# Value products of two softmax attentions: v stationary in column tiles instead of p, with p normalized on GpSimd

## What is computed

```python
# third layer ("wide"): 16 heads of 64
q = (xn @ w_q); k, v = split(context @ w_kv)
scores = einsum('bqhd,bkhd->bhqk', q * SCALE, k)
attn = softmax(scores, axis=-1)
out = einsum('bhqk,bkhd->bqhd', attn, v).reshape(B, SQ, INNER)
out = (out @ w_out + b_out) * tanh(gate[0])
# fourth layer ("narrow"): 16 heads of 16, with a mask
q = query @ Wq.T + bq;  k = key @ Wk.T + bk;  v = value @ Wv.T + bv
scores = where(mask == 0, -1e9, q @ k.T / sqrt(16))
out = softmax(scores) @ v
out = out @ Wo.T + bo
```

## Time and profile before

| | us |
|---|---|
| median of 3 runs | 3672.95 |
| lowest and highest run | 3671.74 and 3675.34 |
| the profiled execution: its own time | 3672.53 |
| the profiled execution: its span | 3670.8 |
| one full wide batch, from scores to scores (1692.84 to 1744.00) | 51.16 |
| one full narrow batch (3101.91 to 3131.27) | 29.36 |

### The profile page before, as it was taken

One profiled execution on the slowest core, in us unless ns is written; L12 is line 12 of the kernel. 1 busy time (PEld: TensorE's weight loads), 2 busy tenths in 40 slices (PEclk: granted clock), 3 DMA queues, 4 the chain that ended last, 5 costly groups with the idle time before them and its releaser, 6 DMA issues. The chain is left out here.

```text
span 3670.8 us, 48289 instructions
## 1 busy us (share of the span) xinstructions
PE 2872.7 (78%) x15310; PEld 2137.1 (58%) x15310; DVE 1500.6 (41%) x5309; ACT 1074.4 (29%) x2159; POOL 292.5 (8%) x338
## 2 busy tenths in 40 slices
PE   4774189996699979699999999927997199999232
PEld 3663167775466745456666666626886077777121
DVE  5886312222211123423333333430111666666777
ACT  3442011110355421033334333302221044444121
POOL 0000300002311100000000000021001211110000
PEclk8896589998799879899999999958998599999555
DMA  2111132211111100100000000025553100000000
GB/s 73 42 48 60 36 139 92 76 61 35 54 34 33 34 30 0 55 9 9 5 8 8 8 8 4 1 88 183 179 180 118 54 26 18 18 18 7 23 0 20
DMA packets 62362, 174.11 MB, mean 47 GB/s; under 512 B 13387, under 2 KB 32601, under 8 KB 52793
## 3 DMA queue, kind: packets, MB, share of 16 engines
q1 hardware_dynamic: 52184, 148.10, 12.2%
q0 software_dynamic: 10080, 24.79, 2.2%
HBM read 143.50 MB, written 29.36 MB: 47 GB/s over the span
## 5 line engine op out<-in xcount | busy, mean ns | idle before, releaser
L2077 PE MATMUL L_ffne_up<-L_ffne_xT,L_ffne_wu 128*128 128x280 f32 (+1 forms) x1696 | 406.1, 398 | 23.1 <-DVE L_ffne_xT L2003 15.6
L2077 PEld LDWEIGHTS L_ffne_up<-L_ffne_xT,L_ffne_wu 128*128 128x128 f32 x1696 | 324.9, 193 | 94.7 <-ACT L_ffne_hT L1990 16.7
L1212 PEld LDWEIGHTS L_xattn_o<-L_xattn_v,L_xattn_pt 125*112 125x112 f32 x3072 | 335.8, 178 | 42.2 <-issue 14.8
L1212 PE MATMUL L_xattn_o<-L_xattn_v,L_xattn_pt 125*112 125x64 f32 (+1 forms) x3072 | 328.2, 251 | 0.0
L1063 DVE TENSOR_REDUCE L_xattn_least<-L_xattn_s 112x1 f32<-112x375 f32 x256 | 128.4, 543 | 473.0 <-PE L_xattn_s L1192 472.8
L2063 PE MATMUL L_ffne_dn<-L_ffne_wd,L_ffne_hT 128*128 128x256 f32 (+1 forms) x1312 | 288.0, 379 | 1.6 <-issue 1.6
L1199 PEld LDWEIGHTS L_xattn_pt<-ident,L_xattn_p 112*125 112x125 f32 x1536 | 186.7, 188 | 138.0 <-issue 138.0
L2063 PEld LDWEIGHTS L_ffne_dn<-L_ffne_wd,L_ffne_hT 128*128 128x128 f32 (+1 forms) x1312 | 240.8, 184 | 44.7 <-issue 2.4
L1147 PE MATMUL L_xattn_job<-L_xattn_ctxT,L_xattn_wk 128*128 128x375 f32 x640 | 233.0, 493 | 2.2 <-DMA L_xattn_msk<-in_mask 1.0
L1076 DVE COPY L_xattn_pt<-L_xattn_pt 125x336 f32<-125x336 f32 x512 | 234.2, 499 | 1.0 <-PE L_xattn_pt L1199 1.0
L1199 PE MATMUL L_xattn_pt<-ident,L_xattn_p 112*125 112x112 f32 x1536 | 232.2, 287 | 0.0
(11 more groups left out here) (318 smaller groups left out, 3875.4 us busy)
## 6 DMA issues: line engine op xcount, KB each, us to landing
L_ffne_wd<-in_L_ffn_down SPq DMA_DIRECT2D x29, 1024.0 KB, 4.9
L_ffne_wu<-in_L_ffn_up SPq DMA_DIRECT2D x21, 1024.0 KB, 5.4
L_ffne_wu<-in_L_ffn_up SPq DMA_DIRECT2D x8, 2048.0 KB, 8.0
L_xattn_ctxT<-in_ctxT SPq DMA_DIRECT2D x32, 375.0 KB, 3.1
fa_ctxT<-in_ctxT SPq DMA_DIRECT2D x16, 375.0 KB, 6.1
fa_rows<-in_ctx_rows SPq DMA_DIRECT2D x16, 375.0 KB
ta_kT<-in_ctxT SPq DMA_DIRECT2D x16, 375.0 KB
ta_ctxr<-in_ctx_rows SPq DMA_DIRECT2D x16, 375.0 KB
```

What stands on the lines that cost most here:

```text
L1212: m = pe.matmul(o, pt_sb[:, head % 4, kt, :], v_sb[:, h, kt, hd, :], start=(kt == 0), stop=(kt == KT - 1))
L2077: m = pe.matmul(up_ps[s % RING][k][:, 0, 0:RH], wu[:, h, c, k * FF + f * 128:k * FF + (f + 1) * 128], xT[:, h, c, q * RH:(q + 1) * RH], st ...
```

## The change

Products are turned round. v of a head is now the stationary operand (125 x 64 in the wide part, 125 x 32 in the narrow part, whose 16 columns are padded with zeros to 32), and `pt` moves with 112 columns. The output of a head is transposed, head columns by queries, and goes to partitions that start at a multiple of 64 or 32: two heads (wide) or four (narrow), `SIDE`, write side by side into column tiles of the array. The tile `o` is then already `onT` for the output projection: `take_o` on ACT copies it, and the transposes of `on` and `head_mean` are gone. As the sum belongs to a query, which is now a column, p is divided before its transpose: the exponential gives the sum, `invert` on DVE takes 1/sum for a pair, and POOL multiplies both heads' p by it, after an instruction on one element. `turn_p` waits for POOL. LT is 4 and LP is 6 (wide) or 8 (narrow), and the rings of p and pt hold 8 heads. In the narrow part `onT` has four chunks of 128 rows instead of two (padding), so the output projection has four matmuls instead of two, and the bias of v goes once through the output projection into `bias_y`.

```diff
-    LT = 2
-    LP = 4
+    LT = 4
+    LP = 6 if wide else 8
+    RP = 8
     if wide:
-        slots = [[K[0]], [K[1]], [K[2], K[3]], [K[4]], [K[5]], [O[0]], [O[1], K[6]], [K[7]], [Y], [Q[0]], [Q[1]],
+        slots = [[K[0]], [K[1]], [K[2]], [K[3]], [K[4]], [K[5], K[6]], [K[7]], [], [Q[0]], [Q[1]], [Y],
                  [V[0]], [V[1], V[2]], [V[3]], [V[4], V[5]], [X]]
     else:
-        slots = [[K[0]], [], [K[1]], [], [Q[0]], [], [O[0]], [], [Y], [], [V[0]], [], [V[1]], [], [X], []]
+        slots = [[K[0]], [], [K[1]], [], [Q[0]], [], [V[0]], [], [V[1]], [], [Y], [], [V[2]], [], [X], []]
...
+                def body(b, h):
+                    for pair in range(0, H, 2):
+                        if pair == 10 and not wide and exists(b + 1):
+                            prepare(b + 1, 1 - h)
+                        pool.wait_ge(rec_done, b * H // 2 + pair // 2 + 1)
+                        pool.tensor_tensor(core.pool_tick[:, pair:pair + 1], ident[0:1, 0:1], ident[0:1, 0:1], ALU.mult)
+                        for head in (pair, pair + 1):
+                            p = pool.tensor_scalar(p_sb[:, head % RP, :], p_sb[:, head % RP, :],
+                                                   rec[:, h, head:head + 1], None, ALU.mult)
+                        p.then_inc(norm_done, 1)
...
+                def take_o(b, w):
+
+                    act.wait_ge(pv_out, b * H + (8 * w + 8 if wide else H))
+                    after(act, out["y"], b)
+                    act.activation(onT[:, 4 * w:4 * w + 4, :], o_ps[:, w if wide else 0, 0:4 * S].rearrange(
+                        "p (c s) -> p c s", c=4), ACT.Copy).then_inc(done["o"], 1)
...
                         exponential(b, h, head + 1)
-                        slot_jobs(job, b, h, head + 1, "kqvxo")
+                        slot_jobs(job, b, h, head + 1, "kqvx")
+                        if head == LP and exists(b - 1):
+                            take_o(b - 1, NO - 1)
+                        if wide and head == 8 + LP:
+                            take_o(b, 0)
...
+                def invert(b, h, pair):
+                    dve.wait_ge(exp_done, b * H + pair + 2)
+                    dve.reciprocal(rec[:, h, pair:pair + 2], sums[:, h, pair:pair + 2]).then_inc(rec_done, 1)
...
                         for head in (pair, pair + 1):
                             lowest(b, h, head)
+                        at, t = behind(b, pair, 2)
+                        if exists(at):
+                            invert(at, h if pair >= 2 else 1 - h, t)
...
                 def turn_p(b, h, head):
-                    pe.wait_ge(exp_done, b * H + head + 1)
+                    if head % 2 == 0:
+                        pe.wait_ge(norm_done, b * H // 2 + head // 2 + 1)
...
                 def products(b, h, head):
-                    pe.wait_ge(pt_done, b * H + head + 1)
+
+                    pe.wait_ge(pt_done, b * H + head + SIDE)
                     if head == 0:
                         pe.wait_ge(done["v"], made("v", b, NV - 1))
-                    if head % 8 == 0:
-                        after(pe, on_done, 2 * b - 1 + head // 8)
-                    hd = head_at(head)
-                    o = o_ps[0:S, hd // 8, (hd % 8) * AV:(hd % 8 + 1) * AV]
+                    if wide and head % 8 == 0:
+                        after(pe, done["o"], 2 * b - 1 + head // 8)
+                    if not wide and head == 0:
+                        after(pe, done["o"], b)
+                    chunk = head // SIDE
                     for kt in range(KT):
-                        m = pe.matmul(o, pt_sb[:, head % 4, kt, :], v_sb[:, h, kt, hd, :],
-                                      start=(kt == 0), stop=(kt == KT - 1))
-                    m.then_inc(pv_out, 1)
+                        for n in range(SIDE):
+                            m = pe.matmul(o_ps[n * VC:(n + 1) * VC, chunk // 4, chunk % 4 * S:(chunk % 4 + 1) * S],
+                                          v_sb[:, h, kt, head_at(head + n), :], pt_sb[:, (head + n) % RP, kt, :],
+                                          start=(kt == 0), stop=(kt == KT - 1))
+                    m.then_inc(pv_out, SIDE)
```

More of the change, by code:

```diff
@@ L1130, in _ @@
                 each_batch(dve, body)
+                invert(NB - 1, 1, H - 2)
                 for head in range(LT):
                     take_pt(NB - 1, 1, H + head - LT)
[L1133 to L1134 removed]
+                c = Chain(dve, chain, start + (NB - 1) * PERB)
                 residual(NB - 1, 1, c)
@@ L1226, in body @@
                         trail(b, h, pair + 1, LT, turn_p)
-                        slot_jobs(job, b, h, pair, "kqvxoy")
-                        trail(b, h, pair, LP, products)
-                        trail(b, h, pair + 1, LP, products)
-                        slot_jobs(job, b, h, pair + 1, "kqvxoy")
+                        slot_jobs(job, b, h, pair, "kqvxy")
+                        if pair % SIDE == 0:
+                            trail(b, h, pair, LP, products)
+                        slot_jobs(job, b, h, pair + 1, "kqvxy")
                 pe.wait_ge(w_in, NLOADS * 16)
+                if not wide:
+                    for c in range(OC):
+                        m = pe.matmul(job_ps[0][0:S, 0, 0:D], bv[:, c:c + 1].broadcast_to([128, S]), wo[:, c, :],
+                                      start=(c == 0), stop=(c == OC - 1))
+                    m.then_inc(bias_out, 1)
+                    pe.wait_ge(bias_done, 1)
                 pe.wait_ge(xn_done, 1)
@@ L1236, in _ @@
                     turn_p(NB - 1, 1, H + head - LT)
-                for head in range(LP):
+                for head in range(0, LP, SIDE):
                     products(NB - 1, 1, H + head - LP)
-                for kind, i in O + [Y]:
-                    job(kind, i, NB, NB - 1, 1)
+                job("y", 0, NB, NB - 1, 1)
 def shared_experts(core):
@@ L2223, in stack_t, with padded @@
         return w.transpose(0, 2, 1).reshape(E, chunks, 128, -1).transpose(0, 2, 1, 3)
+    def padded(w, chunks):
+        n = np.arange(H)
+        head = n // HG * HG + n % HG // 2 + HG // 2 * (n % 2)
+        wide = np.zeros((H, 32, w.shape[1]), np.float32)
+        wide[:, 0:DH] = w.reshape(H, DH, -1)[head]
+        return wide.reshape(chunks, 128, -1).transpose(1, 0, 2)
     ctx = a["ctx_1024"]
```

118 lines of the change are left out of this document (46 added, 72 removed).

## The result

| | us |
|---|---|
| before, median of 4 runs | 3674.1 |
| changed, median of 4 runs (3734.09 to 3745.35) | 3741.6 |
| ratio, 95% interval | 1.0181 (1.0164 to 1.0199) |
| changed, the profiled execution and its span | 3734.09, 3732.4 |

The account below looks back on a forecast made before the run. PE was taken to bound both attentions; wide -30 and narrow -2 us from the profiled 3672.5 gave 3640.5, as a median of runs 3641 us. Likeliest range 3625 to 3660; 8 in 10, 3590 to 3720.

Parts of the forecast that it names:

- What bounds the kernel; products side by side: Both attentions bound by PE; column tiles overlap, so products take 0.76 us (wide) and 0.85 (narrow group), before entering costs.
- 4.9 a batch: Narrow part: gross gain in us from faster products and the dropped job o, less the larger output projection.
- A: Rival, 10%: column tiles don't overlap, each product record costs 0.096 us in turn; total 3791 us.
- A': Rival, 2%: stationary load and matmul of the products run in turn; total 3912 us.
- Wide: -30 us: Wide attention: cheaper products and no transposes of `on` gain 2.15 us a batch, less about 2 in the last.
- The wait for take_o, 1.85 a batch: Narrow pair 8: products wait until ACT, after both exponentials, copies the previous batch's output; 1.85 us lost each batch.
- M: Length of one POOL multiply of narrow p by 1/sum, 375 columns: between 0.40 and 1.48 us, taken as 0.65.
- T': Length of the narrow pair whose transposes need POOL's result; at least 1.5 + 0.25 + 2M - 0.02, 3.03 us, avoids waiting.
- 2.3 a batch: Narrow part: us lost as PE's transposes wait for POOL's multiplies after short pairs.
- The ends: Bias product and its addition, twice the output projection and a longer chain at the narrow tail: an estimated 7 us lost.
- B: Rival, 20%: POOL decides; each 0.1 us more of M adds 12 us, mostly 3665 to 3695, at worst 3771.
- C: Rival, 25%: waits stay small, with M at most 0.5 or groups at 0.76; 3617 us, 3579 without narrow waits.

Follow-up runs that it names:

- run 1: Wide attention as in the changed kernel, narrow attention with the function and inputs of the kernel before; 3644.9 us, ratio 0.993 to the kernel before.
- run 3: Changed kernel with narrow POOL multiplies covering only 168 of 375 columns, 0.699 us each; 3688.7 us, ratio 1.0044 to the kernel before.
- run 2: Changed kernel without the narrow POOL multiplies, so narrow probabilities are not divided by their sum; 3599.7 us, ratio 0.9807 to the kernel before.
- run 8: Changed kernel with narrow transposes 6 and products 10 heads behind the scores, multiplies unchanged; 3619.2 us, ratio 0.9862 to the kernel before.
- run 10: Changed kernel with POOL's preparation of qbd and hide at pair 6 instead of 10, lags unchanged; 3728.6 us, ratio 1.0141 to the kernel before.
- run 11: run 8 with POOL's preparation of qbd and hide at pair 6 instead of 10; 3595.8 us, ratio 0.9778 to the kernel before.

## Why the prediction was wrong

*What bounds the kernel; products side by side.* Right.

```profile
1694.69 0.80 PE L1220 MATMUL L_xattn_o<-L_xattn_pt,L_xattn_v 125*64 125x112 f32 x12
1695.42 2.79 PE L1156 MATMUL L_xattn_job<-L_xattn_ctxT,L_xattn_wk 128*128 128x375 f32 x8
```

Twelve records of the wide part take 0.73 us to the next start where 0.76 was predicted, 24 of the narrow part 0.71 (3121.40 to 3122.11) where 0.85 was. PE's narrow work fell by 79 us; 4.9 a batch was 78. Rivals A and A' are out. A narrow record costs 0.03 us although each needs a load in the same rows of the array as the one ahead of it. By the rule of the Trainium skill ("TensorE: Matmul & The Clock Gate", Part 3) that loads overlap only in another row group, the trace disagrees, as in the prediction.

*Wide: -30 us.* Right: -34 in the stage, -28 in the total of run 1.

*The wait for take_o, 1.85 a batch.* Right in place and nearly in size: 1.58, 14 times.

*The size of M.* This step failed first, and it is worth about half of the miss of 101 us: with a multiply near the assumed length (run 3) 48 of them are left. It reads: "I take 0.65, between the copy and the two-input product, since it reads one tensor and multiplies once". It took 1.228, near the upper bound. The nearest row was the one put aside, the TENSOR_SCALAR of the same shape with 1.482: the same operation weighed less in my choice than the number of inputs. In fact the one-input form is the dearer one on POOL: 0.553 us for 112 columns, 0.699 for 168, 1.228 for 375 are 2.57 ns a column, where the two-input form takes 1.6. The Trainium skill ("GPSIMD Engine Reference", Engine selection) calls one-input work roughly line rate, from which the estimate was 0.5; the trace disagrees.

*"No wait if T' is at least ..."; 2.3 a batch.* The mechanism is right, shown by runs 2, 3 and 8: the wait follows the multiply's length at lag 4 and goes with the lags of run 8. At about the assumed length it came to 23.2 us over the stage, some 1.5 a batch, so 2.3 was not too little. (By its own terms, 1.97 + 0.3 + 0.25 + 0.1 - 0.82, the bound on T' would be 1.8 + 2M and not 1.73; nothing hangs on it.)

*Two terms were missing.* With M near the assumed value, run 3 still gave 3689. The forecast makes a stage of 448 us (457.4 - 11 + 2): some 384 of PE's own work (457.2 less 15 x 4.9) and 64 of waits. Run 3 has 492.0: own work 6 below that figure, idle time 74.5, so 10 above, and 39 of lower clock, for which the sum had nothing. I had read a clock of 1.00 in the kernel before, where PE never waits, and carried it over to a kernel in which I predicted 4 us of waits a batch. And in the idle time stood 26.6 us of a wait that I did not see: the scores of pair 14 behind DVE's residual. (In the changed kernel these two terms are 36.8 and 19.1.) I had weighed POOL's and DVE's shares of time, not that they could obstruct each other. What the rows show is an instruction of 0.294 us that takes 2.13 when it starts behind POOL's, and 0.294 again when the preparation stands elsewhere (run 10). The Trainium skill ("SBUF — State Buffer", Who interferes with whom) says that VectorE and GpSimd have a pair of SBUF ports in common, and that for some forms the one that comes second stands still until the first has ended; the trace agrees, and in it the VectorE instruction stood still over two of POOL's.

*The ends.* Put at 7 us, an estimate. The account has +7.5 between the stages and +6.3 at the tail, 13.8; in the tail PE still waits 4.5 us for POOL.

*The rivals.* B had 20% and is what happened, at a worse point than most of its weight: M beyond 0.9 is slower. Its 12 us for each 0.1 us of M gave 3641 + 69 = 3710 at 1.23. The measured slope between runs is less (540.4 - 492.0 over 0.53 us, 9 for each 0.1); the rest up to 3742 are the two missing terms and the ends. C asked for M at 0.5 or less or for short groups. The short groups came (0.71) and did not keep the waits small by themselves; M was 1.228. Its last figure, 3579 without any wait in the narrow part, was missed by 21 us even with no multiply at all, since the waits for the eviction and for DVE stayed.

*Narrow, in parts.* From the changed kernel's 540.4 to 384.5, in the order in which the edits were made: the lags 114 us, with the multiply unchanged; the multiply's length 1; the preparation's place 40. In another order the multiply is 48 (at lag 4) or 15 (at the end), so these are no fixed shares: each edit pays only once the other waits let it. The 114 hold the wait for the eviction too (run 8).

## What to carry to other kernels

When work moves to an idle engine in the middle of a chain, price the chain's latency against the lags of the loop first, and lengthen every lag behind the new step, the consumer's too. With the right lags the transposes waited 3 us for the same multiplies that had cost 83, and what their length still cost came in the main through a VectorE instruction beside them (run 11). Where an operation has no row, weigh the row of the same operation code: here it was nearer (1.482 for 1.228) than the copy that reads as little (0.40). And every predicted wait on PE needs a second price: what the clock does behind it.
